# A batch pipeline's job tables: offsets of their own for the first four and last two batches, and later loads of the expert weights

## The chip, the core and the metric

The kernel runs on one core of a Trainium2 chip. A core has a matrix engine (PE, with weight loads, PEld, beside it), a vector engine (DVE), a scalar engine (ACT), a general engine (POOL) and a queue engine (SP), which here only issues DMA transfers. Each engine works through its own list of instructions in order and waits on semaphores for the others. The metric is the device time of one execution in microseconds (us), lower is better.

## What is computed

Input x has 32 batches of 256 rows of 256 numbers. Two layers run over it:

```
x = x + xattn0(layernorm(x), ctx)     # correlation over all batches, top 12 lags, one 16-row mix per batch
x = x + moe(layernorm(x))             # 8 experts, each row goes to one: W[e] x + b[e], times its softmax weight
x = x + xattn1(layernorm(x), ctx)     # 16 heads of 16, masked softmax, output product
x = x + ffn(layernorm(x))             # rows quantized to 8 bits, ternary weights, 256 -> 1024 -> 256, gated
```

The correlation of the first step is a mean over all batches, so it must be whole before any batch can go on. The experts' step is done for four batches at a time: the rows of a group of four are sorted by expert, written to memory in that order (scatter), multiplied in 15 tiles of 128 rows, and read back (gather).

## The kernel before

A first stage (to about 113 us) computes the correlation and the mix `attn0_d`. Then one pipeline carries all batches. A *job* is a step of a batch, such as `x2` (x plus the mix), `ln_a` (statistics), `xn_a` (scale and normalize), `xT_a` (transpose), `route` (the experts' scores), `gate` (softmax weight), `sort`, `scatter`, `xs_load` (four sorted tiles back to SBUF), `tile_T` (their transposes), `expert` (product and bias), `y_store`, `gather`, `combine` (makes x3), and then keys, queries, attention (`max`, `exp`, `pv`, `out`, `norm`, `o`) and the feed-forward (`gate_up`, `h_max`, `h_quant`, `h_T`, `down`). Some jobs have chunks (`CHUNKS`): `expert` has two per batch, a *piece* each.

No scheduler runs on the chip. In `pipeline` every engine sorts its jobs by a tick, `n * 128 + AT[job] + LATER[engine][job] + c * apart - lead(job, n, c)`, with n the batch and c the chunk, and the program is written out in that order. So the tables `AT`, `LATER`, `LEAD` and `CHUNKS` set only the order of instructions on each engine, and what an engine does when is left to the semaphores. `lead` is the same for all jobs but those in `TILE_JOBS`, which in the first batches stand later. `BANKS` says which of four shared PSUM banks a job's products use.

What surrounds the change, by line of the kernel before:

- SP's `load_x` (L531 and L534) reads x and the mix of batch n. It waits until batch n-2 is normalized and its x2 is stashed (`stash`, L550, a copy to memory that `x2_back` reads later). With batch 1 it also issues the expert weights (`ew`, 2 MB, L537), with batch 3 the expert biases for all partitions (`eb_r`, 1 MB, L539) and the second zero fill (`zero_rows(1)`, L486, 2 MB): the buffers into which rows are scattered must be zero first. The first zero fill is issued at the end of the first stage.
- POOL makes `x2` (L682), the scales for ACT (L675, L677), the scatters (L694) and gathers (L709), all in one order. Behind the eighth scatter of the first group it fills the stacks `qs` and `ks` (L701, L703). In the steady part it also does `gate_up`'s last product (L716).
- DVE makes the statistics (L931 to L937), the routing (L1015 to L1034), the sort of a group (L1041 to L1064) and, right behind the first group's sort, the ternary weights in nine passes over 128 x 2048 numbers (L996 to L1002).
- ACT normalizes (L829), takes the exponentials of the routing (L840), copies transposes out of PSUM (L835, L847, L920) and the attention output (`out`, L884).
- PE has the transposes `xT_a` (L1425), `route` (L1432), `sort` (L1440, L1443), `tile_T` (L1451) and `expert` (L1466), and all later products.

The tick that orders everything, in both kernels but for the last term:

```
tick = n * TICKS + at + LATER[name].get(job, 0) + c * apart_by - lead(job, n, c)
```

## Time and profile before

| | |
|---|---|
| median of 3 runs | 1541.69 us (1536.97 to 1547.36) |
| the profiled execution | 1532.26 us, span 1530.5 us |
| mean granted PE clock | 0.917 |
| PE busy | 1245.0 us, 81% of the span |
| DVE busy | 1073.6 us, 70% |
| ACT busy | 989.9 us, 65% |
| POOL busy | 703.1 us, 46% |
| chain that ended last | PE 43%, DVE 22%, issue 14%, POOL 7%, DMA 7%, ACT 6% |

And by time, in 40 slices of 38 us, each digit the busy share in tenths:

```profile
PE   5833174788999889989999999989998999888875
DVE  4532532368788888887888788888877778777754
ACT  5722122257777777777777777777767777777674
POOL 4412724235544554455445644564445444444221
DMA  6857255444444554454444454544443444333200
```

A busy share is an average; where PE stands at 9 it leads, and where all stand low each waits for the next. The chain follows the work back from the last instruction, at each step to what released it; "issue" is time in which the engine waited for nothing that the profile shows. The pipeline begins in the fourth slice. Most of its jobs are at rest in slices 3 to 5, and from slice 10 on the picture repeats batch by batch.

### The profile page before, as it was taken

To read this page: it belongs to the slowest core of one execution; us is meant where nothing else is said; L and a number is where in the kernel's file an instruction comes from. 1 tells how busy PE (TensorE), PEld (TensorE's weight loads), DVE (VectorE), ACT (ScalarE), POOL (GpSimd) and SP (SyncE) were. 2 spreads that over 40 slices of the span, in tenths; PEclk is the share of its full clock that TensorE was granted. 3 is DMA by queue.
4 is the path that set the end of the run, shared out by engine and by line. 5 is a ranking of instruction groups with operands and counts; after the bars stand their busy time and mean duration, and the time that the engine had idled before them with its cause. 6 is when DMAs were issued, how large, how long until landed. Compare 5 with 4: busy or idle time off the path is not lost.

```text
span 1530.5 us, 30003 instructions
## 1 busy us (share of the span) xinstructions
PE 1245.0 (81%) x9486; PEld 841.9 (55%) x9486; DVE 1073.6 (70%) x3012; ACT 989.9 (65%) x1910; POOL 703.1 (46%) x886
## 2 busy tenths in 40 slices
PE   5833174788999889989999999989998999888875
PEld 2422163556666666666666666666665666555543
DVE  4532532368788888887888788888877778777754
ACT  5722122257777777777777777777767777777674
POOL 4412724235544554455445644564445444444221
PEclk9975587699999999999999999999999999999896
DMA  6857255444444554454444454544443444333200
GB/s 206 273 174 221 82 162 159 139 141 147 155 152 148 153 161 148 144 158 154 150 151 151 151 154 153 150 142 156 143 139 124 140 147 126 120 106 96 72 8 15
DMA packets 169174, 216.84 MB, mean 142 GB/s; under 512 B 19002, under 2 KB 157628, under 8 KB 162492
## 3 DMA queue, kind: packets, MB, share of 16 engines
q1 hardware_dynamic: 162876, 198.15, 42.3%
q0 software_dynamic: 6144, 16.79, 3.2%
q8 instruction: 79, 1.29, 0.3%
q14 instruction: 75, 0.61, 0.1%
HBM read 133.33 MB, written 79.43 MB: 139 GB/s over the span
## 4 chain that ended last, share of the span: by engine, by line
PE 43%; DVE 22%; issue 14%; POOL 7%; DMA 7%; ACT 6%; SPq 1%; DVEq 0%; POOLq 0%; ACTq 0%
DVE mx L1115 9%; PE mx_pair L1391 5%; PE bank L1466 4%; PE bank L1350 4%; PE ex_pair L1334 4%; PE bank L1418 3%; PE mx_pair L1312 3%; PE bank L1362 3%; DVE small L1171 3%; PE bank L1412 3%; PE mx_pair L1378 3%; PE bank L1474 3%; POOL xs_d L694 2%; DVE t L1166 2%; DVE bn L931 2%
## 5 line engine op out<-in xcount | busy, mean ns | idle before, releaser
L1115 DVE TENSOR_REDUCE mx<-mx_pair 128x4 f32<-128x1024 f32 x256 | 312.6, 1221 | 50.0 <-PE mx_pair L1391 49.4
L716 POOL TENSOR_TENSOR hid<-hid,t 128x256 f32<-128x256 f32 x256 | 196.8, 773 | 216.3 <-DVE t L1166 214.7
L878 ACT ACTIVATE pt<-ex_pair 128x1024 f32<-128x1024 f32 x256 | 262.1, 1024 | 25.9 <-PE ex_pair L1334 25.7
L1391 PE MATMUL mx_pair<-ks,qs 62*128 62x256 f32 x1024 | 132.9, 336 | 69.1 <-DVE mx L1115 63.8
L1350 PE MATMUL bank<-pt,va 128*32 128x256 f32 x2048 | 168.2, 401 | 2.0 <-ACT ot L884 2.0
L903 ACT ACTIVATE hid<-bank 128x256 f32<-128x256 f32 x256 | 98.8, 386 | 105.7 <-PE bank L1362 104.6
L1391 PEld LDWEIGHTS mx_pair<-ks,qs 62*128 62x128 f32 x1024 | 86.0, 197 | 143.5 <-DVE mx L1115 130.5
L1334 PE MATMUL ex_pair<-qs,ks 64*128 64x256 f32 x1024 | 132.3, 337 | 7.8 <-ACT pt L878 7.8
L1466 PE MATMUL bank<-ew,xst 128*128 x480 | 126.9, 409 | 6.3 <-ACT xst L847 6.2
L1166 DVE SCALAR_TENSOR_TENSOR t<-th,bank 128x256 f32<-128x256 f32 x256 | 106.7, 417 | 32.5 <-ACT th L909 22.3
L675 POOL TENSOR_TENSOR rs<-ve,mhalf 128x2 f32<-128x2 f32 x96 | 68.6, 715 | 132.0 <-DVE ve L937 109.6
L729 POOL TENSOR_TENSOR pl<-pf,ph 128x512 fp32r<-128x512 f32 x32 | 40.8, 1275 | 187.0 <-ACT ph L852 186.9
L909 ACT ACTIVATE th<-bank,small 128x256 f32<-128x256 f32 x256 | 121.4, 474 | 0.0
L1334 PEld LDWEIGHTS ex_pair<-qs,ks 64*128 64x128 f32 x1024 | 79.0, 191 | 75.9 <-issue 58.1
L1466 PEld LDWEIGHTS bank<-ew,xst 128*128 128x128 f32 x480 | 94.3, 203 | 28.5 <-issue 15.8
L1362 PE MATMUL bank<-wg,xqt 128*128 128x256 bf16 x512 | 104.8, 288 | 3.0 <-DVE t L1166 1.6
L1362 PE MATMUL bank<-wu,xqt 128*128 128x256 bf16 x512 | 103.5, 286 | 0.0
L694 POOL DMA_INDIRECT xs_d<-xnr,slots x64 | 71.1, 1112 | 48.9 <-DVE slots L1064 27.5
L931 DVE BATCH_NORM_STATS2 bn<-x 128x6 f32<-128x256 f32 x192 | 72.0, 417 | 27.5 <-DMA x<-in_x 24.8
L741 POOL TENSOR_TENSOR pl<-pf,ph 128x512 fp32r<-128x512 f32 x32 | 40.9, 1277 | 104.2 <-ACT ph L863 104.2
L914 ACT ACTIVATE hid<-hid,magic,small 128x1024 f32<-128x1024 f32 x64 | 79.8, 1246 | 6.8 <-DVE small L1178 6.6
L1171 DVE TENSOR_REDUCE small<-hid 128x1 f32<-128x1024 f32 x64 | 77.5, 1212 | 4.2 <-POOL hid L716 4.2
(215 smaller groups left out, 2733.6 us busy)
## 6 DMA issues: line engine op xcount, KB each, us to landing
ks<-ksplit_d SPq DMA_DIRECT2D x192, 128.0 KB
qs<-qsplit_d SPq DMA_DIRECT2D x192, 128.0 KB, 3.1
ys_d<-ys SPq DMA_DIRECT2D x56, 256.0 KB, 2.2
xs<-xs_d SPq DMA_DIRECT2D x24, 512.0 KB, 4.7
x<-in_x SPq DMA_DIRECT2D x32, 256.0 KB, 4.2
va<-in_ctxT SPq DMA_DIRECT2D x32, 256.0 KB, 3.9
xl<-in_x SPq DMA_DIRECT2D x32, 256.0 KB
x_d<-xl SPq DMA_DIRECT2D x32, 256.0 KB, 3.7
```

Source lines behind the costliest of these rows:

```text
L716: pool.tensor_tensor(part_, part_, t1[:, c % 2], ALU.mult).then_inc(hid_made, 1)
L878: act.activation(pt[:, slot:slot + 2].rearrange("p i a c -> p (i a c)"), ex_pair[:, :], ACT.Exp).then_inc(ex_made[u % 2], 1)
L909: act.activation(th[:, c % 2], shared[:, 0:256], ACT.Tanh, scale=ts_[:, c // 4:c // 4 + 1])\
L931: dve.bn_stats(bn[:, i, t], src[:, t]).then_inc(st, 1)
L1115: dve.tensor_reduce(mx[:, t].rearrange("p (r g j) -> p r g j", r=2, j=2)[:, :, g], mx_pair[:, :].rearrange("p (r j s) -> p r j s", r=2, j= ...
L1166: dve.scalar_tensor_tensor(out=t1[:, c % 2], in0=th[:, c % 2], scalar=1.0, in1=shared[:, 0:256], op0=ALU.add, op1=ALU.mult).then_inc(t1_ma ...
L1171: dve.tensor_reduce(hm[:, t:t + 1], hid[:, t], AX_X, ALU.max, apply_absolute_value=True).then_inc(hchain[t], 1)
L1334: ins = pe.matmul(cbanks[r][:, j * S:(j + 1) * S], ks[par][rows, 2 * g + j, key * P:(key + 1) * P], qs[par][rows, 2 * g + j, :], start=Tru ...
L1350: ins = pe.matmul(obank[32 * i:32 * i + 32, 0:S], va[:, par, key, h * 32:h * 32 + 32], pt[:, (2 * u + r) % 4, j], start=(key == 0), stop=( ...
L1362: ins = pe.matmul(shared[:, i * 256:(i + 1) * 256], xqt[:, k, t * P:(t + 1) * P], w[:, k, n * 256:(n + 1) * 256], start=(k == 0), stop=(k ...
L1391: ins = pe.matmul(shared_bank(job, r)[:, j * S:(j + 1) * S], qs[par][rows, 2 * g + j, t * P:(t + 1) * P], ks[par][rows, 2 * g + j, :], sta ...
L1466: ins = pe.matmul(ybank[:, n * D:(n + 1) * D], xst[:, c, n, k], ew[:, k, bass.ds(at, D)], start=(k == 0), stop=(k == KT - 1))
```

## The change

Three things are changed.

*Loads.* The expert weights and biases are issued with `load_x` of batch 5 and the second zero fill with that of batch 7. The waits follow: `first_ld` now counts weights and biases, `late_ld` only the second fill, and the first fill counts on `early_ld`.

*Order.* `pipeline` adds a last term, `edge(job, n, c)`, from two new tables: `FIRST` for batches 0 to 3 and `FINAL` for batches 30 and 31, each with a base, a step per batch and one per chunk. `AT`, `LATER`, `LEAD` and `CHUNKS` have new numbers, too.

*A bank.* The second half of `down` uses shared bank 2 instead of 3.

The diff, cut to its core; of each table a line or two stand:

```
 AT = {
...
-    "load_x": 29, "x2": 193, "stash": 230, "ln_a": 219, "xn_a": 135, "xT_a": 231, "route": 242, "gate": 303,
+    "load_x": 12, "x2": 183, "stash": 240, "ln_a": 221, "xn_a": 135, "xT_a": 231, "route": 242, "gate": 303,
...
-LEAD = {"all": 431, "front": (834, 164), "tiles": (278, 51)}
+LEAD = {"all": 471, "front": (750, 43), "tiles": (281, 47)}
+
+FIRST = {
+    "load_x": (74, -1, 0), "gather": (-10, 5, 3), "x2_back": (-40, -4, 0), "xT_a": (-88, 2, 0),
...
+FINAL = {
+    "max": (0, 8, 0), "down": (2, 4, -13), "out": (-1, -2, 0), "norm": (-5, -2, 2), "h_quant": (-1, 1, -6),
...
-    "norm": [2, 1], "norm_T": [1], "o": [1], "quant_T": [2], "gate_up": [0, 2], "h_T": [1, 0], "down": [3, 3],
...
+    "down": [3, 2],
...
+def edge(job, n, c):
+
+    for table, at in ((FIRST, n), (FINAL, n - NB + 2)):
+        if 0 <= at < (FOUR if table is FIRST else 2) and job in table:
+            base, each, per = table[job]
+            return base + each * at + per * c
+    return 0
...
-                tick = n * TICKS + at + LATER[name].get(job, 0) + c * apart_by - lead(job, n, c)
+                tick = n * TICKS + at + LATER[name].get(job, 0) + c * apart_by - lead(job, n, c) + edge(job, n, c)
...
-                             xn[:, 0].unsqueeze(1).to_broadcast([P, TILES, D])).then_inc((first_ld, late_ld)[i], 16)
+                             xn[:, 0].unsqueeze(1).to_broadcast([P, TILES, D])).then_inc((early_ld, late_ld)[i], 16)
...
-                    if b.n == 1:
+                    if b.n == FOUR + 1:
                         sp.dma_start(ew[:], ewT.rearrange("(k p) n -> p k n", p=P)).then_inc(first_ld, 16)
-                    if b.n == FOUR - 1:
-                        sp.dma_start(eb_r[:], bass.AP(eb.tensor, 0, [[0, P], [1, NE * D]])).then_inc(late_ld, 16)
+                        sp.dma_start(eb_r[:], bass.AP(eb.tensor, 0, [[0, P], [1, NE * D]])).then_inc(first_ld, 16)
+                    if b.n == FOUR + 3:
                         zero_rows(1)
...
-                            pool.wait_ge((first_ld, late_ld)[b.four], 16 * 2)
+                            pool.wait_ge((early_ld, late_ld)[b.four], 16 * (N_EARLY + 1, 1)[b.four])
...
-                            act.wait_ge(first_ld, 16 * 2)
-                            act.wait_ge(late_ld, 16 * 2)
+                            act.wait_ge(early_ld, 16 * (N_EARLY + 1))
+                            act.wait_ge(late_ld, 16)
...
-                            dve.wait_ge(late_ld, 16 * 2)
+                            dve.wait_ge(first_ld, 16 * 2)
```

How the instructions move. Lines of the changed kernel are 39 higher from there on, so `L531` before is `L570` now.

SP's queue in the first batches. `xl<-in_x` and `a<-attn_d` are a batch's load, `x_d<-xl` its stash, `ew` and `eb_r` the expert weights and biases, `xs_d<-xn` a zero fill, `xs<-xs_d` the load of sorted tiles. Before, from the load of batch 1 to the stash of batch 2:

```order
L531 DMA xl<-in_x 128x2x256
L534 DMA a<-attn_d 128x1x256
L537 DMA ew<-in_ewT 128x2x2048
L550 DMA x_d<-xl 128x2x256
L531 DMA xl<-in_x 128x2x256
L534 DMA a<-attn_d 128x1x256
L550 DMA x_d<-xl 128x2x256
L531 DMA xl<-in_x 128x2x256
L534 DMA a<-attn_d 128x1x256
L539 DMA eb_r<-in_eb 128x2048
L486 DMA xs_d<-xn 128x15x256
L550 DMA x_d<-xl 128x2x256
```

And now, from the load of batch 3 on:

```order
L570 DMA xl<-in_x 128x2x256
L573 DMA a<-attn_d 128x1x256
L589 DMA x_d<-xl 128x2x256
L570 DMA xl<-in_x 128x2x256
L573 DMA a<-attn_d 128x1x256
L589 DMA x_d<-xl 128x2x256
L570 DMA xl<-in_x 128x2x256
L573 DMA a<-attn_d 128x1x256
L576 DMA ew<-in_ewT 128x2x2048
L577 DMA eb_r<-in_eb 128x2048
L589 DMA x_d<-xl 128x2x256
L596 DMA xs<-xs_d 128x4x256
```

The weights, the biases and the fill have left the stretch between the loads of batches 1 and 4; weights and biases stand behind the load of batch 5, and the fill behind that of batch 7. The load of sorted tiles comes right behind the stash of batch 4. Before, batch 6's load and batch 5's stash stood between them:

```order
L531 DMA xl<-in_x 128x2x256
L534 DMA a<-attn_d 128x1x256
L550 DMA x_d<-xl 128x2x256
L531 DMA xl<-in_x 128x2x256
L534 DMA a<-attn_d 128x1x256
L550 DMA x_d<-xl 128x2x256
L557 DMA xs<-xs_d 128x4x256
```

The first two rows are batch 5's load and the third is the stash of batch 4; the load of batch 6 and the stash of batch 5 follow, and then the sorted tiles. Now the last row has come ahead of the three above it.

POOL's order around the first scatters. `xl<-xl,a` is a batch's x2, `rs` and `nm` its scale, `xs_d<-xnr,slots` a scatter, `qs` and `ks` the fills. Before:

```order
L682 TENSOR_TENSOR xl<-xl,a 128x512
L675 TENSOR_TENSOR rs<-ve,mhalf 128x2
L677 TENSOR_TENSOR nm<-mneg,rs 128x2
L682 TENSOR_TENSOR xl<-xl,a 128x512
L675 TENSOR_TENSOR rs<-ve,mhalf 128x2
L677 TENSOR_TENSOR nm<-mneg,rs 128x2
L694 DMA xs_d<-xnr,slots 1920x256 x8
L701 MEMSET qs_49 128x2048
L701 MEMSET qs_50 128x2048
L703 CAST ks_51<-nm_rows 128x2048
L682 TENSOR_TENSOR xl<-xl,a 128x512
L675 TENSOR_TENSOR rs<-ve,mhalf 128x2
```

Now:

```order
L721 TENSOR_TENSOR xl<-xl,a 128x512
L714 TENSOR_TENSOR rs<-ve,mhalf 128x2
L716 TENSOR_TENSOR nm<-mneg,rs 128x2
L721 TENSOR_TENSOR xl<-xl,a 128x512
L733 DMA xs_d<-xnr,slots 1920x256 x7
L714 TENSOR_TENSOR rs<-ve,mhalf 128x2
L716 TENSOR_TENSOR nm<-mneg,rs 128x2
L733 DMA xs_d<-xnr,slots 1920x256
L740 MEMSET qs_49 128x2048
L740 MEMSET qs_50 128x2048
L742 CAST ks_51<-nm_rows 128x2048
L721 TENSOR_TENSOR xl<-xl,a 128x512
```

The x2 of batch 5, before behind the fills, stands ahead of the scatters, and its scale between the seventh and the eighth. Higher up, batch 3's x2 has come ahead of batch 2's scale.

ACT's order around the first expert tiles. `xat` is the copy of a batch's transposes, `elg` the routing's exponentials, `xnr` the normalizing, `xst` the copy of a piece's transposes. Before, from the normalizing of batch 5:

```order
L829 ACTIVATE xnr<-xl,nm,rs 128x256 x2
L847 ACTIVATE xst<-bank 128x512
L835 ACTIVATE xat<-mx_pair 128x512
L847 ACTIVATE xst<-bank 128x512
L840 ACTIVATE elg,esum<-lg,ntop 128x8 x2
L829 ACTIVATE xnr<-xl,nm,rs 128x256 x2
L847 ACTIVATE xst<-bank 128x512 x2
L835 ACTIVATE xat<-mx_pair 128x512
L847 ACTIVATE xst<-bank 128x512
```

Now:

```order
L868 ACTIVATE xnr<-xl,nm,rs 128x256 x2
L874 ACTIVATE xat<-mx_pair 128x512
L879 ACTIVATE elg,esum<-lg,ntop 128x8 x2
L886 ACTIVATE xst<-bank 128x512 x2
L868 ACTIVATE xnr<-xl,nm,rs 128x256 x2
L886 ACTIVATE xst<-bank 128x512
L874 ACTIVATE xat<-mx_pair 128x512
L886 ACTIVATE xst<-bank 128x512
L879 ACTIVATE elg,esum<-lg,ntop 128x8 x2
```

Batch 5's copy and exponentials, which stood among the pieces of tile set 0, come ahead of both. On PE, batch 5's route likewise comes ahead of the first piece, batch 6's transposes stand between the transposes and the products of the third piece, and batch 7's between the sixth piece and the seventh instead of behind the seventh.

From the keys of batch 0 on, PE's and DVE's orders are the same in both kernels up to the last batches, but for the bank of `down`. ACT, POOL and SP have a few neighbours exchanged in each batch: on ACT `h_T` of half 0 comes ahead of the last `out`, and the normalizing of a new batch behind `quant`; on POOL both gathers come ahead of the second product of `gate_up`; on SP `x2_back`, the mask load and the stash change places with stores and writes of queries.

## Rows read from the trace of the kernel before

**Rows 1.** busy time by stretch: stretch, us, busy us (x count), clock

```profile
411.60:449.10 37.50, 34.65 (x284) 24.13 (x283) 30.93 (x85) 28.87 (x57) 18.47 (x23) 1.00 0.49 150
...
486.60:564.30 77.70, 69.10 (x569) 47.68 (x568) 63.81 (x183) 57.66 (x113) 44.98 (x53) 1.00 0.50 155
```

**Rows 2.** PE's waits, 564 to 717 us: us in total, times, longest

```profile
PE mx_pair L1391 <- DVE mx L1115: 5.8, 11, 1.4
```

**Rows 3.** the chain that ended last, 116 to 250 us: start us, us, what

```profile
121.94 7.64 DMA x_d<-xl
...
130.70 3.18 DMA x_d<-xl
...
134.36 3.28 DMA a<-attn_d
...
141.30 11.61 issue
...
184.28 1.23 POOL xl L682
...
188.04 0.99 ACT xnr L829 x2
...
236.17 2.40 DMA xs_d<-xnr,slots
```

**Rows 4.** SP's DMA issues from 108 to 262 us: start us, us, line, out<-in

```profile
118.40 0.46 SPq L537 DMA_DIRECT2D ew<-in_ewT  x1
...
135.50 0.43 SPq L486 DMA_DIRECT2D xs_d<-xn  x1
135.98 5.81 SPq L550 DMA_DIRECT2D x_d<-xl  x1
148.47 0.37 SPq L531 DMA_DIRECT2D xl<-in_x  x1
...
185.92 0.47 SPq L557 DMA_DIRECT2D xs<-xs_d  x1
```

**Rows 5.** POOL's timeline from 108 to 262 us, in the same columns

```profile
162.91 8.42 POOL L694 DMA_INDIRECT xs_d<-xnr,slots  x1 [0.30 <-issue]
...
178.88 3.57 POOL L701 MEMSET qs<- 128x2048 f32 x2
```

**Rows 6.** DVE's timeline from 108 to 262 us

```profile
160.01 3.67 DVE L996 TENSOR_SCALAR area<-area,wscale 128x2048 f32<-128x2048 f32 x3
...
169.27 1.22 DVE L1002 TENSOR_SCALAR wd<-area 128x2048 bf16<-128x2048 f32 x1
...
226.22 0.17 DVE L1064 CAST slots<-slotf 128x8 uint32<-128x8 f32 x1
```

**Rows 7.** PE's timeline from 108 to 262 us

```profile
146.07 1.88 PE L1432 MATMUL bank<-rw,xat 128*128 128x8 f32 x8 [0.69 <-ACT xat L835]
...
191.82 3.78 PE L1466 MATMUL bank<-ew,xst 128*128 x8 [0.78 <-ACT xst L847]
...
214.27 1.99 PE L1466 MATMUL bank<-ew,xst 128*128 x8 [0.78 <-ACT xst L847]
...
217.47 1.99 PE L1466 MATMUL bank<-ew,xst 128*128 x8 [0.78 <-ACT xst L847]
```

**Rows 8.** POOL's timeline from 515 to 562 us, where a group of four ends

```profile
544.43 0.73 POOL L716 TENSOR_TENSOR hid<-hid,t 128x256 f32<-128x256 f32 x1
```

**Rows 9.** DVE's timeline from 524 to 560 us, the combine of two gathers

```profile
549.01 0.88 DVE L1085 SCALAR_TENSOR_TENSOR x<-yg,gates,x 128x256 f32<-128x256 f32 x2 [0.99 <-DMA yg<-ys_d,slots]
```

**Rows 10.** ACT's timeline from 612 to 640 us, a batch of the steady stretch

```profile
632.84 0.39 ACT L884 ACTIVATE ot<-bank 128x256 f32<-128x256 f32 x1
633.25 1.02 ACT L920 ACTIVATE hqt<-mx_pair 128x1024 bf16<-128x1024 bf16 x1
```

**Rows 11.** PE's timeline from 601.8 to 640 us, the same batch

```profile
634.90 0.60 PE L1298 MATMUL bank<-ident,ot 128*128 128x128 f32 x4
```

**Rows 12.** DVE's timeline from 1400 to 1532 us, the last batch

```profile
1514.18 1.21 DVE L1171 TENSOR_REDUCE small<-hid 128x1 f32<-128x1024 f32 x1
```

More of the change, by code:

```diff
@@ new lines @@
+LEAD = {"all": 471, "front": (750, 43), "tiles": (281, 47)}
+FIRST = {
+    "load_x": (74, -1, 0), "gather": (-10, 5, 3), "x2_back": (-40, -4, 0), "xT_a": (-88, 2, 0),
+    "xs_load": (-162, 18, 0), "sort": (45, 11, 0), "xn_a": (-119, 29, 0), "max_row": (-33, 11, 0),
+    "ln_a": (-75, -28, 0), "expert": (0, 7, -20), "scatter": (23, 26, 1), "ln_b": (-2, 2, 0), "gate": (38, -16, 0),
+    "x2": (-141, -11, 0), "route": (-47, -1, 0), "v": (2, 0, 0), "stash": (112, -48, 0), "xT_b": (6, -1, 0),
+    "tile_T": (2, 2, -14), "out": (3, -2, -1), "y_store": (-15, -20, 45), "norm": (2, -1, -3), "combine": (-1, 0, 0),
+    "xn_b": (2, -1, 0), "mask": (-17, -7, 0),
+}
```

72 lines of the change are left out of this document (45 added, 27 removed).

## The prediction

> **What bounds the kernel now.** I read the busy time by stretches first, then the chain of waits, then each engine's timeline where the chain stood still. From about 400 us on, one batch takes 37.50 us, of which the matrix engine PE is busy 34.65 at the full granted clock; where a group of four ends, two batches take 77.70 instead of 75 [rows 1]. PE's named waits there are a few for DVE's maxima, 5.8 us in 153 us [rows 2]. So the middle of the kernel, some 28 batches, is PE's work in a fixed order, and only a change of that order or a new wait can move it. The pipeline's start, to about 245 us, is another thing: a relay between queues, in which mostly one engine works and the rest wait. The reader is to see five delays there.
>
> 1. The stash of batch 0's x2 takes 7.64 us to land [rows 3], because 2 MB of expert weights were issued 3.5 us ahead of it [rows 4]; the next one takes 3.18.
> 2. The chain stands 11.61 us from 141.30 [rows 3]. Batch 4's x cannot be loaded until batch 2's stash is down, and that one was issued behind the expert biases and the second zero fill, at 135.98, with 5.81 us for its issue alone, so that the load goes out at 148.47 [rows 4]. DVE has batch 4's statistics ahead of batch 3's routing, so the sort of the first four waits for that load.
> 3. The second scatter takes 8.42 us [rows 5]; it ends 0.9 us after DVE's last ternary weight at 170.4, which began at 160.01 [rows 6].
> 4. The first sorted tiles are loaded at 185.92, behind the stash of batch 5 [rows 4], whose x2 POOL makes only at 184.28 [rows 3], behind its fills, which begin at 178.88 when the last scatter is issued [rows 5].
> 5. Expert pieces go 3.20 us apart (214.27, 217.47) [rows 7], and all but the last piece stand ahead of batch 7's transposes, so the second sort ends at 226.4 [rows 6]. The first gather, x3 and queries all wait for it.
>
> **The change, part by part.** Sums are made against the profiled execution, 1532.3 us (its span is 1530.5); the median of the runs shown is 1541.7, 9.4 above, and I carry the difference in microseconds over.
>
> *Loads moved, first four batches.* Without the weights the first stash lands like the second, after 3.2 us (7.64 - 3.18 = 4.4 sooner). Batch 3's x2 lands at about 133.6: 121.94 + 3.4, a second stash with 3.4, two issues of 0.4 and 3.28 for the small load [rows 3, 4]. But POOL now makes batch 3's x2 ahead of batch 2's scale, so that scale comes at 135, and I give batch 3's scale only 0.7 us, 140.6 for 141.3. From there PE's route 3 ends 6.65 us later (147.95 - 141.30) [rows 7], at 147.25. In the kernel before this lay inside the 11.61 us wait. Behind the wait the path took 7.15 us (152.95 to 160.1); x2 of batch 4 (1.23) is out of it and the sort's products overlap (0.5), so 5.4 stay. The slots are ready at 152.65 for 160.1: 7.5 us gained.
>
> *Scatters and tile load.* Ternary weights and scatters keep their 18.8 us (160.1 to 178.9) [rows 5, 6]. POOL now does batch 5's x2 ahead of them and batch 5's scale between the seventh and eighth, 1.2 us. So the eighth is issued at about 171.4, lands 2.40 later [rows 3], and SP, which has the tile load ahead of batch 6's load and stash 5, issues it at 173.8 for 185.92: 12.1 us gained. The fills come after it and are covered by the load.
>
> *First expert piece.* ACT's order now has batch 5's exponentials ahead of the first tile copy, and DVE's has batch 6's statistics ahead of those. Batch 6's x is issued behind the tile load, 174.8 for its last part, and is there at 178.1 (3.28). From an x2 to the end of its exponentials took 3.76 us (184.28 to 188.04) [rows 3], and copy and handover take 0.75. The first product starts at 182.6 for 191.82 [rows 7]. Here 3 us are lost again; 9.2 are left.
>
> *Tile phase.* From the first product to the second set of slots the kernel before takes 34.6 us (191.82 to 226.4) [rows 6, 7]. Batch 7's transposes stand a piece earlier (3.2), batch 5's route is out of the way (0.9), batch 6's transposes no longer have a gap of their own (1.3): 29.2 us, so the slots come at about 211.8, 14.6 us sooner. The two slow pieces (3.78 us against 1.99 [rows 7]) I leave as they are. The first gather also needs the last expert store; DVE now takes batch 0's keys ahead of the last two expert pieces, and I find the store down at 220 to 226, the gather due at 224. I take **14 us**; bounds 8 (the queue behind the fill, below) and 17 (no slow pieces).
>
> *Steady stretch.* PE and DVE keep their order in it. POOL issues both gathers together: the second goes about 0.6 us earlier, since the product of 0.73 that stood ahead of it (544.43) is now behind it [rows 8] and a short gap between two issues stays. It counts only where DVE idles before the combine, 0.99 us [rows 9], once in each group with a scatter: six times, at most 3.9 us. I take **3**, bounds 0 and 4. The second down product now uses the bank of the values; DVE has read these 2 us before, and in the last batches just in time. On SP, x2_back, the mask load and the stash only trade places with idle time between them. ACT takes h_T of half 0 ahead of the last attention output: 632.84 becomes about 634.2, it ends at 634.55, behind the 1.02 us of h_T [rows 10], and PE needs it at 634.90 [rows 11]. That is free by 0.2 us, with 0.15 for the handover.
>
> *Last batches.* DVE's first maximum of the last batch stands one product earlier, which now is in its way with nothing idle between (1514.18) [rows 12]: 0.4 to 0.8 us; other swaps there trade fractions. **1**, bounds -2 and 3.
>
> Sum: 14 + 3 + 1 = 18 us. 1532.3 - 18 = 1514 for a profiled execution, 1541.7 - 18 = **1524** for the median.
>
> **Rivals.** *Forecast, as above, 0.47*: its own range is gains of 13 to 23, 1519 to 1529.
>
> *The moved loads are in the way again, 0.20.* The zero fill is now issued at about 180.5, ahead of stash 6, and the load of batch 8 and half the expert stores stand behind that stash's landing. In the kernel before, a stash behind fill and biases came down 12.5 us after its issue (135.98 to 148.47) [rows 4]; 9 us, for the fill alone, bring it down at 190, just before it is needed. If it takes the 12.5, the second piece of tile set 1 waits 3 us, and the weights under the scatters may cost as much. For: one queue, the same bytes. Against: they no longer stand before a load that the chain waits for. Gain 10 to 12: 1531.
>
> *POOL's x2 of batch 5 is caught by the ternary work, 0.10.* I place it at 151.4 to 152.7 and the first ternary operation at 152.65. If that operation comes first, x2 waits as the second scatter did, until DVE is through [rows 5, 6], and x2 and the first scatter, 1.3 each, come behind it: 2.6 us, gain 15, 1526. The Trainium skill (SBUF — State Buffer, on the shared port pair) says that whichever of the two engines starts first holds the ports for its whole instruction and the other blocks fully. By that rule only the order of these two starts decides; that the second scatter ended 0.9 us after DVE's last ternary operation agrees.
>
> *The front's gain is given back before the steady stretch, 0.15.* The last expert store, or a mask or key read, is late instead of the slots, and only gathers and end remain: gain 4, 1538. Against: those rows stand idle before the slots' chain arrives.
>
> *Slower than before, 0.05.* The output copy behind h_T reaches PE late. The slack is 0.2 us [rows 10, 11] and the whole h_T is 1.02; if all of it is exposed, each of 29 batches loses 0.8, 23 us, which turns 18 of gain into 5 of loss: 1547. It decides from 0.6 us a batch on. Against: DVE and PE leave h_T ready at 633.2, before ACT is free.
>
> *More than forecast, 0.03*: the front's slow pieces vanish as well, 1516 and less.
>
> **Numbers.** About 1% (15.4 us) is what a measurement of this kernel can tell from no change. A gain above that: most of the forecast's range and half of the ternary case, 0.5 in all with the last one; slower by over 1% needs the slow mechanism and no front gain, 0.04; the rest, 0.46, is within 1%. The range holds everything from a gain of 33 down to 5: 1508 to 1537.
>
> **What would show it.** In the changed kernel's timeline: stash 0 landing 3 to 4 us after issue; first slots at 152 to 154; first tile load at 173 to 175 with no stash ahead of it; first expert product at 182 to 184; second slots at 211 to 214; then batches 37.5 us apart as before. A first scatter that starts after 163, or a stash 6 that lands after 192, speaks for the rivals. A PE wait for the output copy in each batch would make the forecast wrong.

## The result and the profile after

| | before | changed |
|---|---|---|
| median, 20 runs each in one session | 1547.28 us | 1535.25 us |
| range | 1537.0 to 1556.1 | 1527.6 to 1540.3 |
| profiled execution | 1532.26 us, span 1530.5 | 1534.80 us, span 1533.0 |
| granted PE clock, mean | 0.917 | 0.915 |

The ratio is 0.9925, interval 0.9909 to 0.9942: about 12 us gained, 17.7 forecast. One of the twenty runs of before took 3702.4 us; ratio and range leave it out. Against the three runs that the prediction had (1541.69) it is 6.4 us; these three lie 5.6 us below the median of the twenty, and that part of the miss is the starting point, not the change. The predicted 1524 became 1535.

The two profiled executions do not show a gain at all; that of before (1532.26 us) lies below all twenty runs of its kernel. The reader is to see why in two places. First the front. SP's timeline (start us, us, line, out<-in), where [rows 4] had the weights, the fill and 5.81 us for a stash:

```profile
123.27 0.37 SPq L589 DMA_DIRECT2D x_d<-xl  x1
126.89 0.37 SPq L570 DMA_DIRECT2D xl<-in_x  x1
...
139.30 0.37 SPq L570 DMA_DIRECT2D xl<-in_x  x1
...
177.56 0.37 SPq L596 DMA_DIRECT2D xs<-xs_d  x1
...
178.52 0.60 SPq L573 DMA_DIRECT2D a<-attn_d  x1
```

Batch 4's x goes out at 139.30 for 148.47, the first sorted tiles at 177.56 for 185.92. DVE's, POOL's and ACT's timelines of the same stretch, in the same columns with [idle time before <- who ended it]:

```profile
143.52 1.27 DVE L1061 TENSOR_SCALAR ntop<-top 128x2 f32<-128x2 f32 x1
...
154.50 1.14 DVE L1092 TENSOR_TENSOR ones<-upto,iota_t 1x128 f32<-1x128 f32 x1
...
156.13 0.17 DVE L1103 CAST slots<-slotf 128x8 uint32<-128x8 f32 x1
...
216.66 0.17 DVE L1103 CAST slots<-slotf 128x8 uint32<-128x8 f32 x1
```

```profile
143.50 1.26 POOL L721 TENSOR_TENSOR xl<-xl,a 128x512 f32<-128x512 f32 x1 [1.85 <-DMA a<-attn_d]
...
154.23 1.27 POOL L721 TENSOR_TENSOR xl<-xl,a 128x512 f32<-128x512 f32 x1
...
159.11 8.42 POOL L733 DMA_INDIRECT xs_d<-xnr,slots  x1 [0.31 <-issue]
```

```profile
177.63 1.09 ACT L868 ACTIVATE xnr<-xl,nm,rs 128x256 f32<-128x256 f32 x2 [8.53 <-DMA xs_d<-xnr,slots]
```

The slots of the first group come at 156.13 (159.9 before), those of the second at 216.66 for 226.22 [rows 6]. PE's timeline has the first expert product at 187.43 for 191.82, and again two slow pieces [rows 7]:

```profile
187.43 3.78 PE L1505 MATMUL bank<-ew,xst 128*128 x8 [4.03 <-ACT xst L886]
...
192.84 3.78 PE L1505 MATMUL bank<-ew,xst 128*128 x8 [0.78 <-ACT xst L886]
```

In this execution the first `max_T` of PE (maxima of batch 0, my mark for the end of the front) starts at 274.4 for 285.1 before.

Then the steady stretch. Busy time by stretch, in the columns of [rows 1]: the same 37.50 us and the same 34.65 of PE for an ordinary batch, but 81.20 us for 77.70 where a group of four ends:

```profile
402.70:440.20 37.50, 34.65 (x284) 24.15 (x283) 30.93 (x85) 28.98 (x57) 18.28 (x23) 1.00 0.50 150
...
477.70:558.90 81.20, 70.98 (x569) 48.64 (x568) 63.27 (x181) 57.83 (x113) 44.56 (x53) 0.96 0.48 149
```

These 3.5 us sit at one spot. The timeline of PE, ACT, DVE and POOL there:

```profile
523.03 1.03 PE L1417 MATMUL bank<-wd,hqt 128*128 128x256 bf16 x8 [0.57 <-DVE va L1146]
...
527.58 0.40 PE L1359 MATMUL bank<-identb,xq 128*128 128x128 bf16 x4 [0.35 <-issue]
...
531.40 0.96 POOL L733 DMA_INDIRECT xs_d<-xnr,slots  x1 [0.31 <-issue]
532.33 0.60 ACT L936 ACTIVATE xqt<-bank 128x512 bf16<-128x512 bf16 x1 [2.99 <-remote]
...
532.98 0.61 PE L1401 MATMUL bank<-wg,xqt 128*128 128x256 bf16 x2 [2.90 <-issue]
...
533.75 1.23 DVE L1154 TENSOR_REDUCE mx<-mx_pair 128x4 f32<-128x1024 f32 x1 [3.99 <-remote]
```

PE issues the four transposes of the quantized rows (L1359) at 527.58, and they should be over at 527.98. ACT waits for nothing else, and yet its copy (L936) starts at 532.33. DVE's maximum, whose products PE issued at 529.58, starts at 533.75. "remote" is what the profile writes when the semaphore's rise fits no end of an instruction, and so it is here: by the semaphore times of the trace PE's products, which end by the trace at 527.22, 527.98 and 530.08, report done at 529.48, 532.30 and 533.73, the transposes 4.3 us late. I call that a **late completion**. It happens while POOL issues the eight scatters of a group, in all six such batches (4.3, 4.3, 4.3, 4.4, 3.6 and 2.8 us), and nowhere in the first profile of before. A fourth batch takes 43.2 to 45.1 us for 40.2 to 41.7.

### The profile page after: what moved, and what is told of

Read it like the earlier page. It is cut to its first block, busy times and chain, and to the rows that moved or that the text cites. A ratio compares the mean times of both kernels' runs of the same rounds, so it can differ in the third digit from the quotient of the medians.

```text
span 1533.0 us, 30006 instructions
## 1 busy us (share of the span) xinstructions
PE 1248.6 (81%) x9486; PEld 842.4 (55%) x9486; DVE 1074.4 (70%) x3012; ACT 990.4 (65%) x1910; POOL 697.9 (46%) x886
## 4 chain that ended last, share of the span: by engine, by line
PE 47%; DVE 22%; issue 15%; ACT 5%; POOL 5%; DMA 5%; SPq 1%; DVEq 0%; POOLq 0%; ACTq 0%
DVE mx L1154 8%; PE bank L1389 5%; PE mx_pair L1430 5%; PE ex_pair L1373 4%; PE bank L1401 4%; PE bank L1505 4%; PE mx_pair L1351 3%; PE bank L1457 3%; PE bank L1451 3%; DVE small L1210 3%; PE bank L1513 2%; DVE bn L970 2%; DVE t L1205 2%; PE bank L1471 2%; DMA x<-in_x 2%
## 5 line engine op out<-in xcount | busy, mean ns | idle before, releaser
L755 POOL TENSOR_TENSOR hid<-hid,t 128x256 f32<-128x256 f32 x256 | 193.7, 770 | 158.4 <-DVE t L1205 156.8
L768 POOL TENSOR_TENSOR pl<-pf,ph 128x512 fp32r<-128x512 f32 x32 | 40.8, 1274 | 193.3 <-ACT ph L891 193.1
L970 DVE BATCH_NORM_STATS2 bn<-x 128x6 f32<-128x256 f32 x192 | 71.9, 416 | 27.3 <-DMA x<-in_x 24.4
L780 POOL TENSOR_TENSOR pl<-pf,ph 128x512 fp32r<-128x512 f32 x32 | 40.8, 1275 | 94.7 <-ACT ph L902 94.7
```

The source lines that it names most:

```text
L755: pool.tensor_tensor(part_, part_, t1[:, c % 2], ALU.mult).then_inc(hid_made, 1)
L970: dve.bn_stats(bn[:, i, t], src[:, t]).then_inc(st, 1)
```

## Experiments

18 experiments ran in five jobs, each job on one chip beside runs of the kernel before; jobs 2 and 5 had the same chip, so there are four chips. Which chip the first session had is not on record. Each edit is to the changed kernel unless told otherwise. Ratios are to the kernel before of the same job. The lateness is that of the transposes (L1359) in the six fourth batches; where the record of a report is missing, it is taken from the start of ACT's copy.

| kernel | us (median) | ratio, interval | lateness in the profile |
|---|---|---|---|
| job 1: e1, changed kernel | 1518.57 | 0.9878, 0.9852 to 0.9904 | none |
| e2, only the front | 1525.67 | 0.9945, 0.9923 to 0.9967 | none |
| e3, bank back | 1514.81 | 0.9871, 0.9845 to 0.9898 | none |
| e4, xnr back | 1516.65 | 0.9881, 0.9858 to 0.9904 | none |
| job 2: e5, kernel before | 1543.36 | 0.9990, 0.9967 to 1.0013 | 0.5 to 2.6 |
| e6, only the loads | 1544.13 | 0.9995, 0.9974 to 1.0015 | 1.1 to 3.3 |
| e7, only the orders | 1537.03 | 0.9955, 0.9936 to 0.9974 | 1.5 to 4.3 |
| e8, six xnr buffers | 1532.80 | 0.9926, 0.9902 to 0.9950 | 1.4 to 5.8 |
| job 3: e9, changed kernel | 1537.32 | 0.9924, 0.9897 to 0.9952 | 1.4 to 4.3 |
| e10, sort behind | 1539.10 | 0.9941, 0.9921 to 0.9962 | 6.2 to 6.5 |
| e11, plain scatters | 1509.51 | 0.9771, 0.9734 to 0.9807 | none |
| e12, no FINAL | 1536.82 | 0.9948, 0.9922 to 0.9974 | 1.4 to 4.3 |
| job 4: e13, before, plain scatters | 1523.28 | 0.9852, 0.9818 to 0.9885 | none |
| e14, changed, plain scatters | 1508.93 | 0.9763, 0.9732 to 0.9795 | none |
| e15, plain in every other group | 1520.13 | 0.9835, 0.9792 to 0.9878 | 3.7 to 4.4 in the indirect ones |
| e16, changed kernel | 1533.61 | 0.9921, 0.9896 to 0.9946 | 1.5 to 4.4 |
| job 5: e17, bank and xnr back | 1526.54 | 0.9863, 0.9829 to 0.9898 | 0.5 to 2.8 |
| e18, sort behind, again | 1540.44 | 0.9970, 0.9947 to 0.9993 | 6.3 to 6.5 |

### Does the loss return? (e1, e9, e16: no edit)

> The changed kernel, unchanged, for its spread and a second profile. In its first profile the max_T of batch 2 stands 12.3 us ahead of before, and then every fourth batch (3, 7, 11, 15, 19, 23) gives back 1.4 to 3.9 us, about 17 in all; in six of them VectorE's maximum and ScalarE's copy of the transposed quantized row stand idle 1.9 to 4.0 us at the same time. Theory A (that loss belongs to the order): it returns in the same six batches with the same sizes, and the ratio is 0.990 to 0.995. Theory B (that loss was one of that execution only): a profile without it, some 15 us shorter than 1533.

Measured: none of the six late completions, a span of 1517.1 us for 1533.0, ratio 0.9878. The same instructions, ACT, DVE and PE, in that profile's timeline:

```profile
526.54 0.40 PE L1359 MATMUL bank<-identb,xq 128*128 128x128 bf16 x4 [0.36 <-DVE xq L1198]
...
528.21 0.58 ACT L936 ACTIVATE xqt<-bank 128x512 bf16<-128x512 bf16 x1
...
529.15 0.61 PE L1401 MATMUL bank<-wg,xqt 128*128 128x256 bf16 x2
529.26 1.23 DVE L1154 TENSOR_REDUCE mx<-mx_pair 128x4 f32<-128x1024 f32 x1 [0.53 <-PE mx_pair L1430]
```

PE's transposes to ACT's copy take 1.67 us here and 4.75 there, in one and the same program. Neither theory was whole: the loss is not the order's alone, and not of one execution, as the next runs show.

> The changed kernel, unchanged, as the neighbour of the next three on their chip. Two chips so far: on one its fourth batches hold matrix products whose completion is recorded 2.8 to 4.4 us late (ratio 0.9925), on the other none (0.9878). A theory on the chip (the pause belongs to the chip, before has it there too) expects one of these two pictures, the same in all six fourth batches up to the last; a theory of chance within a chip expects single ones.

On a third chip all six are late again, ratio 0.9924, and so it was on a fourth:

> The changed kernel, unchanged, beside e13 to e15 on their chip. With late completions in its profile: ratio 0.991 to 0.994; without: 0.986 to 0.989.

Measured 0.9921 with late completions. So the picture goes with the chip. The four profiles of job 1's chip have no late completion; all those on the three other chips have them where the scatters are indirect. The changed kernel itself has 0.9878 on the former and 0.9921 to 0.9925 elsewhere. There is one more mark: of the 6250 semaphore updates that the engines' instructions should make, the traces of job 1 lack 0 to 4, those of the three other chips 89 to 182. The first profile of before lacks 3 and that of the changed kernel 183. So the two first profiles are probably not of one kind of chip, and their difference is then not the change alone. Whether the profiler, which loses these records, also has a part in the lateness is not shown.

### Parts of the steady order, on the chip without late completions (e2, e3, e4)

e2 takes tick, spacing and banks from before for all batches from 4 on, and its end:

```diff
+                if n >= FOUR:
+                    tick = (n * TICKS + MID_AT[job] + MID_LATER[name].get(job, 0)
+                            + c * MID_CHUNKS.get(job, (1, 0))[1] - LEAD["all"])
```

> The offsets of the first four batches and the later loads as changed, but from batch 4 on the offsets, the spacing and the banks of before, and its end: one part alone. Theory A (the steady order of the change makes the loss of every fourth batch): the loss goes and the front's 11 to 12 us stay, so some 15 us faster than the changed kernel: ratio to before 0.980 to 0.987, and no idle time over 1 us ahead of the copy of the quantized row in batches 7, 11, 15, 19, 23. Theory B (a longer or denser run of TensorE, reached by the earlier start, brings it, whatever the order): it stays, ratio 0.990 to 0.995.

Measured: 0.9945, no lateness to lose. The first max_T stands at 272.2, so the front's gain is all there, but batches 3, 4, 5 and 7 take 1.0 to 1.8 us each more than in e1 and the end from batch 23 on 3.1 us more. So on this chip e2 is some 7 to 10 us slower than e1, mostly where the front hands over and at the end. The first part need not be the steady tables' worth: at batch 4 e2 joins the new tables to the old ones, an order that neither kernel has. For the theories on the late completions the run says nothing.

```diff
-    "down": [3, 2],
+    "down": [3, 3],
```

> The changed kernel with the second down product back in bank 3 instead of bank 2, nothing else. Theory A1 (the bank: TensorE waits 0.57 us for the values' addition ahead of down in every fourth batch, and what follows runs into the pause): the pauses of 2 to 4 us go, 10 to 17 us faster than the changed kernel, ratio to before 0.981 to 0.987. Theory A2 (another part of the steady order): at most 6 times 0.5 us, 3 us faster than the changed kernel, ratio 0.989 to 0.994, and the pauses stay.

```diff
+                if name == "act" and job == "xn_a" and n >= FOUR:
+                    tick -= 23
```

> The changed kernel with ScalarE's normalization of the front (xnr) from batch 4 on back where it stood, ahead of h_T and absmax instead of behind quant. Theory A3 (its two activations of 1.09 us behind quant come into the scatter's time and hold the row that follows): the idle time ahead of the quantized row's copy goes from 3.0 to below 1 us in every fourth batch, 10 to 17 us faster than the changed kernel. Theory A2: within 3 us of the changed kernel, ratio to before 0.989 to 0.995.

Measured 0.9871 and 0.9881 beside e1's 0.9878: no difference that can be told. In their profiles the bank alone moves PE's transposes (L1359) back from 6.20 to 6.42 us behind the first scatter (e3), and the xnr alone ACT's copy of them from 7.87 to 7.49 us behind it (e4). With nothing late, theories A1 to A3 could not be parted here; e17 does it.

### The kernel before once more (e5)

> The kernel before, unchanged, for a second profile of it beside the changed one's second (e1_after_again). Theory D (the two records of before differ in the middle): batches 4 to 23 of this profile hold some us more than the first one's, in the fourth batches or in single ones, since the runs of before lie between 1525 and 1556 us and the first profile was among the shortest. Theory E (the difference sits in the front alone): batches 4 to 31 within 2 us of the first profile, and the first max_T away from 285.1 by the rest. Ratio 1.000 within 0.003.

Theory D. The span is 1545.4 us, and before has late completions too, only shorter. From this profile's timeline of PE, ACT and DVE:

```profile
541.88 0.40 PE L1320 MATMUL bank<-identb,xq 128*128 128x128 bf16 x4
...
544.92 0.60 ACT L897 ACTIVATE xqt<-bank 128x512 bf16<-128x512 bf16 x1 [1.88 <-remote]
546.36 1.22 DVE L1115 TENSOR_REDUCE mx<-mx_pair 128x4 f32<-128x1024 f32 x1 [2.53 <-remote]
```

From batch 0's max_T to batch 23's it needs 898.8 us, and 886.4 in the profile that I had predicted from. That profile was one without late completions.

### The front's parts (e6, e7, e8)

e6 is the kernel before with the diff's part on the loads alone; e7 the changed kernel with the loads at their old places:

```diff
-                    if b.n == FOUR + 1:
+                    if b.n == 1:
                         sp.dma_start(ew[:], ...)
+                    if b.n == FOUR - 1:
                         sp.dma_start(eb_r[:], ...)
-                    if b.n == FOUR + 3:
                         zero_rows(1)
```

> The kernel before with only the loads moved: expert weights and biases issued behind batch 5's load, the second zero fill behind batch 7's, all offsets as before. By the prediction's first step the loads alone carry the slots' 7.5 us: first slots at 152 to 155 us (160.1 before), first max_T 6 to 9 us sooner than 285.1, ratio 0.993 to 0.996. The rival (the moved loads stand in the way again where the old order has batch 5 and 7's loads): slots sooner by as much, but the first max_T by 0 to 3 us, ratio 0.997 to 1.001.

Measured: slots at 155.44, the first product at 187.36, the second slots at 223.58, the first max_T at 282.5, ratio 0.9995. It is the rival: 4.5 us gained at the first slots, 2.7 left at the first max_T, and nothing measurable in the time. In SP's timeline the tile loads stand behind stashes again, one of which takes 3.13 us to issue behind the fill:

```profile
181.07 0.36 SPq L550 DMA_DIRECT2D x_d<-xl  x1
181.47 0.47 SPq L557 DMA_DIRECT2D xs<-xs_d  x1
...
186.15 3.13 SPq L550 DMA_DIRECT2D x_d<-xl  x1
...
189.32 1.28 SPq L557 DMA_DIRECT2D xs<-xs_d  x1
```

> The changed kernel with the loads issued where they stood: weights behind batch 1's load, biases and second zero fill behind batch 3's. Theory L (the loads carry the first slots, the orders the tile phase): stash 0 lands 7 us after its issue again, the slots come at 158 to 161, and 5 to 7 us of the front's 12 are gone: ratio 0.991 to 0.994. Theory O (the orders carry nearly all, the fill only fills a wait that they took away): slots before 156, ratio as the changed kernel's 0.988 within 0.002.

Measured: slots at 158.16, second slots at 216.6, first max_T at 275.3, ratio 0.9955. The ratio lies above the range of either theory. The slots are theory L's, but the orders alone bring 9.8 of the front's 10.7 to 12.5 us: the tile phase earns it, not the first slots.

e8 gives xnr a sixth buffer:

```diff
-XN = 5
+XN = 6
-        mk = over("mk", 15872, [P, 2, S], I32)
+        mk = sb("mk", [P, 2, S], I32)
```

> The changed kernel with six instead of five buffers for the normalized front rows (the mask buffer leaves their area for one of its own). In the changed kernel ScalarE's normalization of batch 5 stands 8.5 us until the first group's scatters have landed, since it writes batch 0's buffer, and the first expert product comes at 187.4 for the 182.6 forecast. If that wait is what the prediction missed: no wait ahead of xnr of batch 5 (starts at 170 to 172 instead of 177.6), first expert product at 182 to 184, first max_T 3 to 5 us sooner, ratio to before 0.984 to 0.987. If the load of the sorted tiles or batch 6's x2 is late by itself: product at 186 to 188, ratio as the changed kernel's.

Its timeline:

```profile
174.90 1.09 ACT L868 ACTIVATE xnr<-xl,nm,rs 128x256 f32<-128x256 f32 x2 [5.84 <-POOL nm L716]
...
187.21 3.78 PE L1505 MATMUL bank<-ew,xst 128*128 x8 [4.73 <-ACT xst L886]
```

The wait for the scatters is gone, ACT now waits for POOL's scale, which stands between the seventh and eighth scatter (174.66), and the product still comes at 187.21. The second alternative holds: batch 6's x2 waits for its load (182.8), and with DVE and ACT in their order everything behind it. A real wait, worth nothing.

### What makes the completions late (e10, e18, e11, e15)

e10 puts the sort on DVE behind the third LayerNorm's statistics and the first scatter behind the norm's scale:

```diff
+BEHIND = {("dve", "sort"): 7.5, ("pool", "scatter"): 3}
+                if n >= FOUR and (name, job) in BEHIND:
+                    tick += BEHIND[name, job]
```

> The changed kernel with the sort behind the third LayerNorm's statistics on VectorE and the first scatter behind the norm's scale on GpSimd, from batch 4 on. In e1's fourth batch the sort (2.2 us) and the first scatter (1.1) stand ahead of these, ScalarE waits 4.09 us for the scale, and the batch takes 41 us for 37.5. If these two set the fourth batch: ScalarE's wait falls to about 1 us, the values come 1 us sooner, the batch takes 38 to 39 us, seven times 2 to 3 us, ratio to before 0.975 to 0.980 without pauses. If the pause is brought by TensorE's idle time there, it also shrinks. If something else (the late slots, POOL behind the scatters) sets it: 41 us as before and the changed kernel's ratio.

```profile
516.34 1.12 POOL L737 DMA_INDIRECT xs_d<-xnr,slots  x1 [1.46 <-DVE slots L1107]
...
521.18 0.40 PE L1363 MATMUL bank<-identb,xq 128*128 128x128 bf16 x4
...
525.56 0.96 POOL L737 DMA_INDIRECT xs_d<-xnr,slots  x1 [0.30 <-issue]
527.81 0.60 ACT L940 ACTIVATE xqt<-bank 128x512 bf16<-128x512 bf16 x1 [4.20 <-remote]
```

PE does come earlier: its transposes are issued 4.8 us after the first scatter, 6.2 in the changed kernel's first profile. But they are now 6.2 us late, and ACT starts 11.5 us after the first scatter, 10.95 there. The fourth batches take 44.3 to 44.7 us. What PE gains under the scatters is taken back by lateness. The expectation that the lateness shrinks with PE's idle time fell: it grew. Whether the order of sort and first scatter sets the fourth batch could not be read under it.

> The kernel of e10 once more. With late completions in its profile: 6.2 us late, as there, ratio 0.992 to 0.996. Without: fourth batches of 38 to 39 us for 41, ratio 0.972 to 0.980, which would make it the fastest of all on such a chip.

Measured: late again by 6.3 to 6.5 us, 0.9970, a little slower than the 0.992 to 0.996 that I expected. What this order gives on a chip without late completions was not to be seen.

```diff
+                    if b.four >= 1:
+                        pool.dma_start(xs_d[b.four % 2][c * P:(c + 1) * P],
+                                       xnr[:, (FOUR * b.four + c // T) % XN, c % T]).then_inc(sc_dma[b.four % 2], 16)
+                        return
```

> Leaves the sorting of rows out from the second group on: the scatters go out as plain DMAs of the same 128 rows and bytes to fixed rows, so that the experts read unsorted rows. Theory I (the indirect transfers or GpSimd's making of them bring the late completions and hold GpSimd 1.27 us each): no late completions on a chip that has them in its neighbours, and fourth batches of 37.5 to 40 us. Theory T (it is TensorE's own doing, from what it does before and after): the same late completions and 41 us or more a batch.

Measured: nothing late, fourth batches of 38.9 to 40.8 us, beside e9, e10 and e12, which are all late on this chip. It is the picture of theory I. (The kernels with plain scatters leave out the sorting of the rows, so that they compute something else.) e15 asks the same within one execution, with `if b.four % 2` in place of `>= 1`:

> The changed kernel with plain scatters in the second, fourth, sixth and eighth group only (batches 7, 15, 23, 31), indirect ones in the third, fifth and seventh (11, 19, 27); leaves out the sorting in the former. Theory I (the indirect scatters make TensorE's completions late): on a chip that has them, late completions of 3 to 4 us in the batches 11 and 19 and 43.5 to 45 us for them, none in 3, 7, 15 and 23 and 39 to 41 us there (batch 3 holds the second group's scatter). If the records are late in neighbouring groups too, it is not the transfer itself.

```profile
519.81 3.78 POOL L734 DMA_DIRECT2D xs_d<-xnr  x7
...
523.89 0.40 PE L1363 MATMUL bank<-identb,xq 128*128 128x128 bf16 x4 [0.30 <-DVE xq L1202]
...
525.63 0.57 ACT L940 ACTIVATE xqt<-bank 128x512 bf16<-128x512 bf16 x1
...
679.16 0.40 PE L1363 MATMUL bank<-identb,xq 128*128 128x128 bf16 x4 [0.37 <-issue]
...
682.98 0.96 POOL L737 DMA_INDIRECT xs_d<-xnr,slots  x1 [0.30 <-issue]
683.92 0.60 ACT L940 ACTIVATE xqt<-bank 128x512 bf16<-128x512 bf16 x1 [3.01 <-remote]
```

1.7 us from the transposes to the copy beside plain scatters, 4.8 beside indirect ones, and so in turn through all six groups: late by 4.4, 4.3 and 3.7 us in the three indirect ones, not at all in the three between. (The scatters of the second group fall into no such batch; I had named the batches by one group too early, so that batch 3 is late where I expected none.) One thing differs beside the indices: the plain scatters are over sooner, seven in 3.78 us for 8.7 and all eight in 5.65 us for 10.97, so PE's transposes come just behind them. The five products that PE ends under them (`down` to `pv`, 520.6 to 523.6) report on time by the trace's semaphore times, but they decide little: of the same five in the indirect groups of this execution, those that end up to 5.26 us behind the first scatter are on time where their reports are recorded, and only `pv`, at 5.83 us, is late (by 2.99 us in the first). In other kernels some that end earlier are late, too: `pv` at 1.07 us by 0.4 us in e5, and in e10 every one recorded from 1.94 us on, by 0.9 us and more. So the lateness comes with a run of indirect scatters and goes when they are plain. Whether the indices bring it, or that POOL's run of issues is twice as long, was not parted, nor by what path it holds PE's reports.

### Do they take more from the changed kernel? (e13, e14, e17)

e13 is e11's edit in the kernel before, e14 is e11 once more.

> The kernel before, with the sorting of rows left out from the second group on: scatters as plain DMAs of the same 128 rows to fixed rows, experts read unsorted rows. With e14 it asks what the change is worth where no indirect scatter runs in the steady batches. Theory J (the late completions take 4 to 7 us more from the changed kernel than from before, that is what the forecast lacks): before gains less by this edit than the changed kernel does (23 to 28 us): 14 to 20 us, ratio 0.987 to 0.991. Theory K (they take the same from both, the missing gain is elsewhere): ratio 0.982 to 0.985, and e14 stands 11 to 12 us below this run.

> The changed kernel with the same left out (as e11, for more executions beside e13). Theory J: 16 to 20 us below e13, the forecast's 18; ratio to before 0.975 to 0.979. Theory K: 11 to 12 us below e13.

By ratio the edit, which also frees POOL for some 5 us a group, is worth 22.9 us to before and 24.4 to the changed kernel (0.9921 to 0.9763), and e14 stands 14.4 us below e13: between the 11 to 12 of theory K and the 16 to 20 of theory J, with an interval that holds both. Before's 0.9852 is where theory K had it (0.982 to 0.985) and not where theory J did (0.987 to 0.991), and e14's 0.9763 is theory J's. By totals the question stays open. The two single edits decide more, taken back together on a chip that has late completions:

> The changed kernel with two steady edits taken back at once: down's second product in bank 3 and ScalarE's xnr ahead of h_T. On a chip with late completions the changed kernel needs 899.8 to 905.8 us from batch 0's max_T to batch 23's, the kernel before 898.8 to 901.6. If these two edits are what the steady stretch loses there: 897 to 900 us and completions at most 2.7 us late, ratio 0.988 to 0.991. If not: 900 to 905 and the changed kernel's ratio, 0.992. On a chip without them: within 2 us of 887.6 either way.

Measured: 1526.54 us, ratio 0.9863, the six transposes at most 2.8 us late, much as in the kernel before, and 894.6 us from batch 0's max_T to batch 23's. In its timeline:

```profile
521.87 1.05 PE L1419 MATMUL mx_pair<-wd,hqt 128*128 128x256 bf16 x8
...
527.28 0.40 PE L1361 MATMUL bank<-identb,xq 128*128 128x128 bf16 x4
...
530.42 0.60 ACT L938 ACTIVATE xqt<-bank 128x512 bf16<-128x512 bf16 x1 [1.99 <-remote]
```

`down` no longer waits for the values, and the copy comes 9.6 us after the first scatter, for 10.95. This kernel beats both: 0.9863 (0.9829 to 0.9898) where the changed kernel had 0.9921 to 0.9925 on three occasions, and on the chip of job 1 each of its two edits alone costs nothing. The comparison is across jobs, and the interval just touches those of e9 and e16; e8 (0.9926, 0.9902 to 0.9950), the changed kernel but for a buffer that proved worth nothing, is of the same chip. Which of the two edits does it was not parted on such a chip. The time from max_T to max_T is not the clean proof, since e7, with the steady order of the change, has 897.6 us and e6, with that of before, 901.7. The lateness is: at most 2.8 us here, 2.6 in e5 and 3.3 in e6; in each of the six profiles with the steady order of the change and late completions it reaches 4.3 us or more.

### The last batches (e12)

```diff
-    for table, at in ((FIRST, n), (FINAL, n - NB + 2)):
+    for table, at in ((FIRST, n),):
```

> The changed kernel without the offsets of the last two batches: one part of the change alone taken back. The prediction priced them at 1 us, bounds -2 to 3; the two profiles of the changed kernel need 65.5 and 66.9 us from the last max_T to the end, those of before 68.6 and 67.9. If the offsets carry that: 68 us here, 1 to 3 us slower than the changed kernel on the same chip. If it is the steady order: 65 to 67.

From the last max_T to the end it takes 69.8 us, but that max_T comes earlier by as much; from batch 23's to the end it is 354.8 us beside e9's 355.1. 0.9948 beside 0.9924 is 3.7 us slower, within the intervals, and by the medians it is 0.5 us faster. The offsets of the last two batches are worth between nothing and 4 us, and the trace shows no gain.

## Why the prediction was right or wrong

Starts of max_T and the end of the last instruction that computes, from the traces:

| | first max_T | to batch 23's | from there to the end |
|---|---|---|---|
| before: first profile; e5 | 285.1; 286.5 | 886.4; 898.8 (late) | 356.3; 357.5 |
| changed: e1 (none late) | 273.3 | 887.5 | 353.6 |
| changed: first profile, e9, e16 (late) | 274.4, 272.6, 273.4 | 901.7, 905.9, 899.8 | 354.4, 355.1, 354.5 |
| e17 (late) | 274.8 | 894.6 | 355.0 |

**The front, 14 us: nearly right.** The means of the first max_T are 285.8 and 273.4, 12.4 us. The working held step by step with small losses: the stash landed 3.6 us after issue (3.2 forecast), batch 4's load went out at 139.3 (137), the slots came at 156.1 (152.65), tiles at 177.6 (173.8), the product at 187.4 (182.6), the second slots at 216.7 (211.8). In the first profile the pipeline also began 1.4 us later. Of the 3.5 us at the slots, DVE gave two: its small operations at 143.52 and 154.50 take 1.27 and 1.14 us, where the same lines take 0.17 and 0.27 when POOL is silent, and POOL's x2 had started 0.02 and 0.27 us ahead of them and ended 0.03 and 0.14 us before they did. By the rule of the Trainium skill that I had weighed for another place (SBUF — State Buffer, on the shared port pair) the engine that starts first blocks the other for its whole instruction, where DVE's is of a kind that takes the shared ports. By it POOL blocked DVE here, and the trace agrees. The case that I priced by it, x2 of batch 5 caught by the ternary work, did not come: 154.23 was ahead of it. The 4.8 us at the product are the 3.7 that the tile load was late already and the load of batch 6 behind it: issued at 178.52 and there at 183.02, 4.5 us where I had 3.28. (The terms that I gave for batch 3's x2 add up to 132.8 us, not 133.6; no later step hangs on it.) I also missed ACT's wait of 8.53 us for the scatters, a full ring of five buffers; e8 showed that it hid behind the same load.

**The loads' share: wrong.** I gave the slots 7.5 us to the loads. Alone they gain 4.5 there and nothing in the time (e6), because the old order puts the tile load behind the stashes; the rival of the moved loads is true of the loads alone, and the orders keep it off (e7: 9.8 us without the loads).

**The steady stretch, +3: the step that failed.** Two errors. The gathers' gain did not come, although the idle time of [rows 9] is gone. DVE's combine in e1's timeline has none ahead of it:

```profile
539.46 0.87 DVE L1124 SCALAR_TENSOR_TENSOR x<-yg,gates,x 128x256 f32<-128x256 f32 x2
```

And yet the six fourth batches take 246.2 us together in e1 for 247.0 in the first profile of before, and batch 7 alone 40.56 for 40.19. A wait of an engine in the middle of a batch was no wait of the batch. And I costed the bank at nothing and did not price ACT's xnr, moved from ahead of h_T to behind quant, at all. Without late completions both are nearly free. The first two batches behind the front differ by up to 3.3 us from one profile to the next of one kernel; from batch 2's max_T to batch 23's e1 needs 809.3 us, e3 and e4 810.0 and 808.1, the first profile of before 809.7.

With late completions the stretch loses: 902.5 us on average, for 898.8 in e5 and 901.7 in e6 (the order of before), and e17, without these two, has 894.6. From batch 2's max_T on, the six profiles with the steady order of the change need 823.7 to 828.3 us, e5, e6 and e17 820.2, 824.1 and 819.5. That is 3 to 4 us on average, with ranges that overlap a little, so the sign is likely and the size is rough. In the fourth batch PE waits 0.57 us for the values ahead of `down`. The product before the transposes ends 5.84 us behind the first scatter in the changed kernel's first profile and 6.49 in e17, the transposes are issued at 6.20 and 6.42, and they are up to 4.4 and 2.8 us late; in e10, issued at 4.84, they are up to 6.5 late. The sooner they run under the scatters, the later they report. Of PE's waits ([rows 2]) I had read one row; a second one, of `max_T` itself, is nearly as large:

```profile
PE mx_pair L1398 <- DVE mx L1115: 4.7, 4, 1.2
```

I could not have read the lateness from that profile; that its place, the fourth batch, had no slack, I could.

**The end, 1: low.** 356.9 and 354.4 on average, 2.5 us.

**The sum.** 12.4 - 3.7 + 2.5 = 11.2 us with late completions (902.5 against e5's 898.8), against 12 measured; 12.4 - 1.1 + 2.5 = 13.8 without. The spans of e1 and of the first profile of before agree with the latter (1530.5 - 1517.1 = 13.4), but e1's runs beside those of before on their chip say 18.7 (14.7 to 22.7). So on the chip without late completions the forecast's 18 lies within what the runs measured, though not by its terms; with them it is half as much again as the 12 measured. The other 5.6 us of the miss are the three runs of before that I carried the gain over to.

**The rivals.** The output copy behind h_T cost nothing: ordinary batches stay 37.50 us. The front was not given back before the steady stretch, but in it.

## What to carry to other kernels

Price a reordering against the stretches that have the least slack, here every fourth batch, and count an operation that merely ends up later there as a cost, even where the trace shows its place idle. A single profile of before can be one of a chip or execution that lacks a loss which others have: when it is 9 us below the median of its own runs, ask what those have more. And an idle time that a change removes is a gain only if the chain of waits runs through it.

## What the hardware showed

On three of four chips PE's completions are late while POOL issues a run of eight indirect scatters of 128 rows of 1 KB each, most of them 1.27 us apart. The transposes that fall under the run report 0.5 to 5.8 us late, most often near 1.2, 2.7 or 4.3 us, and up to 6.5 us where PE's work came earlier under the scatters (e10, e18). ACT and DVE report on time. With plain DMAs of the same bytes, over in half the time, it is gone, in alternate groups of one execution (e15). The granted clock is low (0.5, the 1.2 GHz level) for 6.8 to 10.2 us around it in the changed kernel's first profile and for 3.4 us at the same spots in e1, where nothing is late. But it is low for 6.8 us at five of the six in the first profile of before, too, where nothing is late either; which of lateness and clock follows the other the records do not tell. The Trainium skill (TensorE: Matmul & The Clock Gate, on the cost of a semaphore per tile) says that the increments of products that each raise a semaphore serialize, at some 26 ns each. The reports here are 1.4 and 2.8 us apart (529.48, 532.30, 533.73), fifty times that and more, and no run here shows whether it is the same path.

The two gathers of each batch, which are indirect too, two at a time, had no late completions beside them. And the second scatter of the first group takes 8.42 to 8.44 us in all 20 profiles. In each of them DVE's nine passes for the ternary weights run beside it and it ends 0.84 to 0.86 us after the last of them, where most scatters take 0.96 us. No run here moved the two apart.
